# Constant rows for the projection and gate biases, and x in nine transfers, in a graph layer with a routed feed-forward

## What is computed

```python
x = x + gnn(layernorm(x), adj, nodemask)
x = x + ffn(layernorm(x))

# gnn
h = einsum('bni,di->bnd', x, W) + b
logits = (h @ a1)[:, :, None] + (h @ a2)[:, None, :] + att_b
att = sigmoid(logits) * adj * mask[:, :, None] * mask[:, None, :]
att = att / (sum(att, axis=-1, keepdims=True) + 1e-8)
h_new = einsum('bij,bjd->bid', att, h) * mask[:, :, None]

# ffn
gate_logits = x @ gate_w + gate_b
topk_vals, topk_idx = top_k(gate_logits, 2)
moe = sum over the two chosen experts of softmax weight * (relu(x @ w1 + b1) @ w2 + b2)
return layernorm(x + moe) * gamma + beta
```

## Time and profile before

| | us |
|---|---|
| median of 3 runs | 518.03 |
| the three runs | 511.93, 518.03, 519.29 |
| span of the profiled execution, first to last instruction | 512.2 |
| the profiled execution's own time beside its span | not given by the page; nothing outside the span is shown |
| TensorE busy | 343.2 (67%) |
| GpSimd busy | 340.2 (66%) |
| VectorE busy | 328.7 (64%) |
| ScalarE busy | 271.1 (53%) |

### The profile page before, as it was taken

How to read it: one execution, slowest core, us unless ns; L and a number is a source line. 1 busy time by engine, 2 the same in 40 slices (tenths; PEclk the granted TensorE clock), 3 DMA queues, 4 the chain that set the end, 5 groups by cost and what they waited for, 6 DMA issues and landing times.

```text
span 512.2 us, 11792 instructions
## 1 busy us (share of the span) xinstructions
PE 343.2 (67%) x2282; PEld 288.9 (56%) x2283; DVE 328.7 (64%) x1628; ACT 271.1 (53%) x726; POOL 340.2 (66%) x360
## 2 busy tenths in 40 slices
PE   2689999999999662008979888888887888000000
PEld 1458787778777562007969777767776777000000
DVE  3745898978988874203756756565566555159992
ACT  2345887877876632104655555555555555026552
POOL 3522077777777777651777777777777777727884
PEclk9999999989999965557998999999999999655555
DMA  6711333433433311756766655555555550097843
GB/s 188 210 51 54 104 106 110 150 104 104 150 112 106 116 52 54 167 117 188 201 203 185 183 176 166 182 172 165 178 177 178 172 175 8 0 284 205 262 129 105
DMA packets 67530, 73.60 MB, mean 144 GB/s; under 512 B 10035, under 2 KB 61821, under 8 KB 67508
## 3 DMA queue, kind: packets, MB, share of 16 engines
q1 hardware_dynamic: 45028, 46.89, 32.3%
q0 software_dynamic: 9216, 17.01, 10.0%
q10 hardware_dynamic: 13264, 9.46, 6.7%
HBM read 49.86 MB, written 25.55 MB: 147 GB/s over the span
## 4 chain that ended last, share of the span: by engine, by line
issue 28%; POOL 22%; PE 21%; DVE 11%; DMA 7%; ACT 6%; ACTq 3%; POOLq 1%; DVEq 1%; SPq 0%
POOL token_y L380 12%; POOL sorted_x L358 9%; DMA token_y<-yb,y_row 4%; PE psum L1036 3%; PE psum L1035 3%; PE psum L1053 3%; ACT z L549 2%; PE psum L1132 2%; DVE rs L951 2%; PE psum L1043 2%; PE psum L1023 2%; PE psum L1142 2%; DMA sorted_x<-xrow,rows 1%; PE psum L1071 1%; ACTq L406 1%
## 5 line engine op out<-in xcount | busy, mean ns | idle before, releaser
L380 POOL DMA_INDIRECT token_y<-yb,y_row x160 | 158.5, 991 | 62.1 <-issue 45.1
L358 POOL DMA_INDIRECT sorted_x<-xrow,rows x128 | 123.0, 961 | 61.9 <-issue 40.3
L521 ACT ACTIVATE hid<-psum,wb 128x256 f32<-128x256 f32 x160 | 67.2, 471 | 113.5 <-PE psum L1132 113.5
L1132 PE MATMUL psum<-xbT,wb 128*128 128x256 f32 x320 | 90.7, 407 | 26.5 <-DVE xbT L878 26.4
L1142 PEld LDWEIGHTS psum<-w,hid 128*128 128x128 f32 x640 | 85.2, 194 | 5.1 <-issue 0.8
L1142 PE MATMUL psum<-w,hid 128*128 x640 | 85.6, 277 | 0.4 <-DVE yb L893 0.4
L886 DVE TENSOR_TENSOR yb<-psum,wb 128x256 f32<-128x256 f32 x80 | 34.0, 424 | 80.6 <-DMA token_y<-yb,y_row 71.8
L1132 PEld LDWEIGHTS psum<-xbT,wb 128*128 128x128 f32 x320 | 55.9, 195 | 43.3 <-DVE xbT L878 38.5
L527 ACT ACTIVATE x_first<-xb 128x128 f32<-128x128 f32 x160 | 55.0, 397 | 0.0
L893 DVE SCALAR_TENSOR_TENSOR yb<-yb,xb,x_first 128x128 f32<-128x128 f32 x160 | 49.3, 349 | 0.5
L878 DVE COPY xbT<-psum 128x256 f32<-128x256 f32 x80 | 33.4, 417 | 24.2 <-PE psum L1124 24.2
(11 more groups left out here) (134 smaller groups left out, 579.9 us busy)
## 6 DMA issues: line engine op xcount, KB each, us to landing
wb<-experts_dram SPq DMA_DIRECT2D x80, 193.0 KB
xb<-sorted_x SPq DMA_DIRECT2D x80, 131.0 KB
adj_in<-adj_dram SPq DMA_DIRECT2D x32, 256.0 KB
got<-token_y SPq DMA_DIRECT2D x16, 512.0 KB, 4.1
out_dram<-res ACTq DMA_DIRECT2D x16, 256.0 KB, 2.5
token_y<-yb,y_row POOLq DMA_INDIRECT x160
w<-experts_dram SPq DMA_DIRECT2D x16, 128.0 KB
sorted_x<-xrow,rows POOLq DMA_INDIRECT x128
```

Source lines behind the costliest of these rows:

```text
L358: pool.indirect_dma_start(sorted_x, bass.IndirectOffsetOnAxis(ap=rows[:, slot, t, k:k + 1], axis=0), xrow[:, slot, k, t, :], None).then_in ...
L380: pool.indirect_dma_start(token_y, bass.IndirectOffsetOnAxis(ap=y_row[:, q, t:t + 1], axis=0), yb[:, q, t, :], None, bounds_check=TOKENS * ...
L521: last = act.activation(hid[:, q % RING, c, :], psum[:, 2 + q % 2, c * BT:(c + 1) * BT], ACT.Relu, bias=wb[:, q, B1 + c:B1 + c + 1])
L1132: last = mm(psum[:, 2 + q % 2, c * BT:(c + 1) * BT], wb[:, q, c * P:(c + 1) * P], xbT[:, q % RING, :], start=True, stop=True)
```

## The change

- **Biases.** Since a normalised row sums to zero, the last column of it is minus the sum of the others. The kernel now leaves row 127 of the transposed tiles `xnT` and `xn2T` at a constant 1 (GpSimd fills both tiles with ones at the start, ScalarE copies rows 0 to 126 only), subtracts the weights' last row from the other rows, and puts the bias in row 127 of `w_aug` and of `gate_aug`. The bias product of each tile and the addition of `gate_b` on VectorE go; the largest two are now searched in PSUM. `w_aug` comes from a product of `w_less` with the identity, extended by a column for a2, plus a product of one row.
- **x** comes in nine transfers (4, 4 and seven of 8 tiles); ScalarE issues the first three at once at the start, SyncE the other six, behind the late weights and ahead of w2 and of the loop that loads adjacency.
- **Statistics.** The nine chunks are spread over the first turns of VectorE: 0 to 4 ahead of turn 0, 5 and 6 ahead of turn 1, 7 ahead of turn 2, 8 ahead of turn 3.
- **Smaller.** ScalarE does a one-column sigmoid at the start; the adjacency of pair 0 is transposed right behind `transpose_x(0)`; the Newton steps need one `var_eps` instead of two, with another constant for the guess.

```diff
-XCHUNKS = ((0, 4), (4, 16), (16, 32), (32, 48), (48, 64))
+XCHUNKS = ((0, 4), (4, 8)) + tuple((lo, lo + 8) for lo in range(8, TILES, 8))
+EARLY_X = 3
...
@@ sync
-            for dst, src in ((gate_w_sb[:, :], gate_w), (gate_b_bc[:, :], gate_b.partition_broadcast(P)),
+            for dst, src in ((gate_w_sb[:, :], gate_w), (gate_last[:, :], gate_w[D - 1, :].partition_broadcast(P)),
+                             (gate_b_bc[:, :], gate_b.partition_broadcast(P)),
...
+            for c in range(EARLY_X, len(XCHUNKS)):
+                load_x(sp, c)
             load_w2(0)
@@ gpsimd
+            g.memset(xnT[:, :], 1.0).then_inc(const_done, 1)
+            g.memset(xn2T[:, :], 1.0).then_inc(const_done, 1)
@@ scalar
-            load_x(0)
-            act.wait_ge(weights_in, 16 * 6)
-            load_x(1)
+            for c in range(EARLY_X):
+                load_x(act, c)
...
-                act.copy(xn2T[:, :], xT_ps).then_inc(x2T_copied, 1)
+                act.copy(xn2T[0:D - 1, :], xT_ps[0:D - 1, :]).then_inc(x2T_copied, 1)
...
-                act.copy(xnT[:, :], xT_ps).then_inc(xT_copied, 1)
+                act.copy(xnT[0:D - 1, :], xT_ps[0:D - 1, :]).then_inc(xT_copied, 1)
...
-            act.wait_ge(const_done, 13)
+            act.wait_ge(const_done, 15)
+            act.activation(warm[:, :], eps_t[:, :], ACT.Sigmoid)
             norm1(0)
-            for c in range(2, len(XCHUNKS)):
-                load_x(c)
             transposed(0)
@@ vector
+                v.tensor_scalar(w_less[:, :], w_raw[:, :], w_raw[:, D - 1:D], None, ALU.subtract).then_inc(setup_dve, 1)
...
+                dve.wait_ge(setup_pe, 3)
+                v.tensor_copy(w_aug[:, :], psum[:, 0, 0:HA]).then_inc(setup_dve, 1)
...
+            def setup_gate():
+
+                dve.wait_ge(late_in, 16 * 5)
+                n = step(v.tensor_tensor(gate_aug[:, 0, :], gate_w_sb[:, :], gate_last[:, :], ALU.subtract))
+                dve.wait_ge(dve_step, n)
+                v.scalar_tensor_tensor(out=gate_aug[:, 1, :], in0=gate_b_bc[:, :], scalar=ident[:, D - 1:D],
+                                       in1=gate_aug[:, 0, :], op0=ALU.mult, op1=ALU.add).then_inc(gate_ready, 1)
...
-                    n = step(v.tensor_scalar(var_eps[:, 0, :], mv2[:, :, 1], EPS, None, ALU.add))
-                    step(v.tensor_scalar(var_eps[:, 1, :], mv2[:, :, 1], EPS, -0.5, ALU.add, ALU.mult))
+                    n = step(v.tensor_scalar(var_eps[:, :], mv2[:, :, 1], EPS, -0.5, ALU.add, ALU.mult))
...
-            def gate_logits(i):
+            def largest(i):
                 dve.wait_ge(gate_done, i + 1)
-                n = step(v.tensor_tensor(logits[:, :, :], gate_v, gate_b_bc[:, None, :].broadcast_to([P, TPP, EXPERTS]),
-                                         ALU.add))
-                return n
...
             stats_of(0)
-            setup()
-            for c in range(1, len(XCHUNKS) - 1):
+            setup_weights()
+            stats_of(1)
+            setup_projection()
+            for c in (2, 3):
                 stats_of(c)
+            setup_gate()
+            stats_of(4)
             turn(0, 0)
-            stats_of(len(XCHUNKS) - 1)
+            for c in (5, 6):
+                stats_of(c)
             turn(1, 1)
+            stats_of(7)
             turn(2, 0)
+            stats_of(8)
@@ tensor
-            pe.wait_ge(const_done, 13)
-            pe.wait_ge(setup_dve, 4)
-            tr(psum[:, 0, 0:P], w_raw[:, :], ident[:, :])
-            mm(psum[:, 0, P:P + 1], w_raw[:, :], vec[:, 1:2], start=True, stop=True)
...
+            mm(psum[:, 0, 0:HA], w_less[:, :], ident_aug[:, :], start=True, stop=False)
             pe.wait_ge(setup_dve, 8)
+            mm(psum[:, 0, 0:HA], e_last[:, :], h_bias[:, :], start=False, stop=True).then_inc(setup_pe, 1)
+            pe.wait_ge(setup_dve, 10)
...
-                    mm(h_v[:, t, :], xnT[:, c:c + P], w_aug[:, :], start=True, stop=False)
-                    last = mm(h_v[:, t, :], ones_f[0:1, :], h_bias[:, :], start=False, stop=True)
+                    last = mm(h_v[:, t, :], xnT[:, c:c + P], w_aug[:, :], start=True, stop=True)
...
-                if valid(m):
+                if valid(m) and begun(m):
                     transpose_adj(m)
...
             transpose_x(0)
+            transpose_adj(0)
```

66 lines of the change are left out of this document (36 added, 30 removed).

## The result

The changed kernel takes 498.97 us (median of four runs, 496.88 to 500.44), the kernel before in the same comparison 515.17 (four runs, 511.93 to 519.29): a ratio of 0.972, 95% interval 0.969 to 0.976. It is faster: by 16.2 us between the two medians, by 12.6 to 16.2 us by the interval of the ratio. The forecast was 506.0 with a range from 500.0 to 512.5: the sign and the way were right, the time came out 7.0 us lower, 1 us under the range.

The account below looks back on a forecast made before the run. GpSimd's unbroken scatters were taken as the bound, so only an earlier first scatter counts: 10.9 us from the chain plus 1.2 from TensorE's clock, 512.2 − 12.1 = 500.1 span, plus 5.8 around it, 506 us; range 500 to 512.5.

Parts of the forecast that it names:

- The frame: Phase 1: GpSimd's last scatter comes a fixed 162.7 us after its first; only shifting the first scatter counts.
- signs that I had named for being wrong: Scatter spacing other than 1.27, GpSimd waits between pairs, TensorE awaiting `w_aug` beyond 10 us, 0.73 us products beyond 30.
- biases up to the aggregation: products: TensorE, pairs 0 and 1: eight bias products of 0.73 us leave the chain, 5.84 us gained.
- the same: earlier rate: TensorE before the first aggregation's end: rate doubles near 25 us instead of after the aggregation, 1.2 us gained.
- shorter stretch to `rows` without them: First aggregation to `rows`: fewer VectorE waits for adjacency transposes (2.2 us) and three small operations fewer (0.4).
- table 2.4: ScalarE's start: one table load hidden, one gone, twice 1.28 us less 0.2 for `w_aug` ahead of the transposes.
- weights −0.5: TensorE's start: weights may land late behind early x chunks, 0.5 us lost, between 0 and 1.5.
- x 4.2: ScalarE's start: large x transfers no longer stand between the first transposes and their copy, 4.2 us gained.
- adjacency 0.8: Pair 0's adjacency transposes leave the chain (1.90) but add 1.1 before the first projection, net 0.8 us gained.
- statistics −4.4: VectorE, first aggregation to first scatter: statistics of eight tiles twice now stand on the chain, 4.4 us lost.
- Late rate or late data: Rival: TensorE slow until 32 us or beyond, or adjacency 1 late; gain only 5 to 10 us, 509.5; chance 0.27.
- GpSimd starves: Rival, scatter loop: longer gaps keep TensorE at its lower clock, turns take 13.0 us, time 547; chance 0.05.

Follow-up runs that it names:

- zero products put back: Changed kernel plus a product adding zeros per projection product: one row 652.97 us, 128 rows 649.31, one-row products grouped 653.77.
- weights first: Changed kernel, but ScalarE issues x chunks 1 and 2 only once the weights have landed: 639.0 us (one run).
- late statistics alone: Changed kernel with statistics of chunks 7 and 8 moved ahead of VectorE's turns 5 and 7, inverse deviations on VectorE: 493.96 us, ratio to before 0.965.
- no table load ahead: Changed kernel without the one-column sigmoid at ScalarE's start: 500.06 us (one run), beside 498.71 for the changed kernel.
- adjacency back in its turn: Changed kernel with pair 0's adjacency transposes back in turn 0 instead of right behind `transpose_x(0)`: 650.64 us (one run).
- statistics all early: Changed kernel with statistics of chunks 7 and 8 ahead of turn 1, beside 5 and 6: 641.56 us (one run).
- the kernel with both edits: Late-statistics kernel, x chunks 1 and 2 issued after the weights land, projection's small operations ahead of chunk 1's statistics: 641.29 us, ratio to before 0.962.

## Why the forecast was right, and where it was short

**The frame held.** The time of the first scatter plus a fixed rest: the first scatter moved by 15.2 us, the span by 17.1 (15.4 in the second trace of the changed kernel, 496.8 us), and in the second session four kernels with first scatters from 43.66 to 50.43 have 447.8 to 448.6 us from there to the end. GpSimd is fed throughout; pair 1 came 9.6 us after pair 0, where I had called 9.5 an upper bound and 10.1 the need. The frame is one of a loop in which GpSimd issues without a pause; in the other two sessions it doesn't, and there the scatters take 225.4 to 227.2 us with the changed kernel's products and 229.6 to 233.5 with the zero products put back. Of the signs that I had named for being wrong, one came: TensorE waited for `w_aug` beyond 10 us, until 11.32.

**Term by term**, against the sum of 12.1:

| term | forecast, us | shown |
|---|---|---|
| biases up to the aggregation: products | 5.84 | 7.7 |
| the same: earlier rate | 1.2 | 2.3 |
| shorter stretch to `rows` without them | 2.6 | 2.9 |
| all else together (table 2.4, weights −0.5, x 4.2, adjacency 0.8, statistics −4.4) | 2.5 | 2.3 |
| sum | 12.1 | 15.2 |

The first three are the kernel with the biases alone (10.05 and 2.9; of the 10.05, 8.0 are at the projections, of which 0.3 by the rate in one half); the fourth is the difference between it and the changed kernel. Of the 2.6 I had put 1.4 down to the lead that TensorE gains during the statistics; the kernel with the biases alone has the statistics as before and got 2.9 without that. The miss of 3.1 us is in the biases: 1.9 in the products, 1.1 in the rate, 0.3 in the stretch to `rows`, less 0.2 elsewhere. The step that failed is "eight of 0.73 lie on this chain: 5.84 us"; it measured 7.7. It took from a row what one product costs and assumed that its neighbour stays as it is. The neighbour's 0.73 (0.80 in the earlier trace rows) held 0.3 us of weight load that one row behind 128 had laid bare. The clue stood in the old trace: four transposes of 128 columns, one record each, take 1.09 us, so two records of about that size should take some 0.5, not 0.73.

**The clock.** The reason was right (with products of one row the rate doubles at 36 us, with 128 rows near 17, with nothing changed in the kernel but the rows; that the exposed weight loads have a share in it is not excluded), the moment was not: I had TensorE resume at 20 and rise at 25, while with the adjacency in front it works from 8.27 on and rises near 15. "Adjacency, net 0.8" can't be judged closely: the run with it back came 2.1 us later at the first scatter, weights apart, and 0.7 or 1.8 us at the first aggregation, as it is held against the one or the other trace with the adjacency in front.

**Tables, x, weights, statistics.** The table was 2.4 and measures 2.3, though one of the two loads (1.28 us) was hidden anyway; the rest came from the low rate behind the longer wait, so the size was met by luck. x from ScalarE was 4.2 and measures 3.9 at the projection and 6.0 at the first scatter. The rule of the Trainium skill ("DMA: Bandwidth & Descriptors", Issuing engines are not separate DMA queues), that all a move to another engine saves is the sequencer's time to start the transfer, usually small beside the transfer itself, is not borne out by that trace: three issues of 512 KB each took 5.01 us there, about as long as moving them takes at the 302 to 317 GB/s of that stretch (an estimate). The late weights I had at 0.5, at most 1.5: they cost 2.0 at the transposes (11.32 against 9.29 with weights first and the projection's operations ahead) and landing first brought nothing at the first scatter, since x then lands later and VectorE waits for that instead. What late weights alone cost there, where VectorE stood 1.93 us for them (the copy at 7.42), is not shown. The statistics were 4.4 and measure 4.5. Taken out one by one these terms don't add up: 2.3 for the table, 6.0 for x and 2.1 for the adjacency, less 4.5 for the statistics, make 5.9 us at the first scatter, and all together they gave 2.3. Why is not shown; VectorE is the bound in the changed kernel, so one term may hide behind another. That my 2.5 came so near is luck.

**PSUM.** I took 0 for the search in PSUM, and an estimate by the Trainium skill ("VectorE: DVE Perf Modes", The TRN2 errata) would have given 0.5 us. In the changed kernel four MAX8 out of PSUM take 0.42 us, in the kernel before 0.41 out of SBUF. The trace decides for 0.

**From span to time.** The forecast's span was 500.1 and came out 495.1: 3.1 from the first scatter, 0.5 from the scatters and 1.4 behind them. The last two are one execution's: in the second trace of the changed kernel the span was 496.8 us, and 3.1 of the 3.3 us missed there are the first scatter's. To the span I added 5.8 us for what lies around it. In the profiled executions of all the other kernels the time lies 1.7 to 2.0 us above the span, in two of them 3; the rest of my 5.8 was that the profiled execution, by that some 514 us, was a shorter one and the median of three, 518.03, happened to be high (515.17 with a fourth run). By this slip the forecast was 4 us too high: without it the same working gives 501.9, 2.9 above what was measured. The changed kernel's profiled execution was 2.1 us under its own median, which took back part: 5.0 + 4.0 − 2.1, about the 7.0 missed.

**The rivals.** *Late rate or late data*: no, the rate came early; the weights were late, but by 2 us, and the adjacency of pair 1 wasn't. *GpSimd starves*: its mechanism is there. A pair had eight products of 0.41 us and has four of 0.22 now, 2.4 us less, 24 in ten pairs; TensorE's busy time falls by 11.7 only, and the granted clock to 0.90 and 0.81. The other half went back with the lower granted clock, as far as these rows tell. It didn't decide: GpSimd's busy time in the same windows is unchanged to 0.01 us.

## What to carry to other kernels

Before you price a product that is to go, look at its neighbours: a product of few rows between products of 128 costs its own time, the weight load that it lays bare in the next one, and the rate that TensorE would have risen to; a constant row in the operand does the same work without a product of its own. When one engine issues without a pause to the end of a phase, only what stands ahead of its first issue counts: take out of that stretch all that is needed only later (the late statistics alone brought 4.6 us), and ask which engine is late there before you speed up another. And add to a forecast span only what other executions show around theirs, not the distance to a median.

## What the runs showed of the hardware that I had not expected

- A change from 128 rows to one or back keeps the next weight load from being hidden: products of 130 columns follow each other every 0.73 us at the low rate and 0.41 at the high one when they alternate, every 0.43 and 0.22 with 128 rows throughout, and 2.19 us for four in groups of two. The Trainium skill ("TensorE: Matmul & The Clock Gate", Part 3, The mechanism) says in its list that a weight load overlaps running products only where the groups of rows differ, and above it that a load into the background buffer is pulled ahead too; here it overlaps where all 128 rows stay the same and not where one row follows 128.
- With products of one row in between, the high rate comes late. TensorE at work from 8.4 to 8.8 us on: rate doubled at 36 us with alternating one-row products, at 27.5 with grouped ones, near 17 with 128 rows. The granted clock reads 1.00 over all of these stretches, so the length of like products is the view to trust there.
- A short wait can cost more than itself: behind a wait of 2.95 us (no table load ahead), 1.98 (adjacency back in its turn), 1.97 (weights first) and 1.70 (statistics all early) TensorE works at the low rate again for some 3 us, and the granted clock over 20 to 24 us reads 0.57 to 0.71. Behind 1.53 or 1.54 in four traces (the changed kernel's, at 19.22, among them) and 1.85 in the run with 128-row products (at 20.93) it did not. So the length of the wait alone doesn't decide it; what does is not shown.
- In two of three sessions the loop of phase 1 took longer; in the trace of the kernel with both edits GpSimd stands 4.4 to 6.0 us ahead of every eighth scatter, put down to "issue" or to `rows`, where it waits 0.3 in the second session. The granted clock was lower there, 0.74 to 0.77 over the span instead of 0.84. What caused it stays open, as does the break in pair 14, which is in every trace (1.9 to 2.2 us).
